# The residual sum of the attention split between ScalarE and POOL, with a new order of turn, copy and normalisation in each slot

## The reference

```
x = x + L0_xattn(layernorm(x), ctx, ctx)      # 16 heads of 8, biases, plain softmax
x = x + L0_ffn(layernorm(x))                  # 8 experts, each token goes to its top one
x = x + L1_xattn(layernorm(x), ctx, ctx)      # position bias per head, exp / (1 + sum)
x = x + L1_ffn(layernorm(x))                  # relu squared, two products, 5 spiking steps
```

## Time and profile before

| what | value |
|---|---|
| median of three executions | 414.28 us (412.43 to 416.89) |
| profiled execution | 411.08 us, span 409.3 us |
| TensorE matmul busy | 304.5 us, 74% |
| VectorE busy | 288.0 us, 70% |
| ScalarE busy | 253.5 us, 62% |
| POOL busy | 166.5 us, 41% |
| mean granted TensorE clock | 0.888 |

### The profile page before, as it was taken

One profiled execution on the slowest core, in us unless ns is written; L12 is line 12 of the kernel. 1 busy time (PEld: TensorE's weight loads), 2 busy tenths in 40 slices (PEclk: granted clock), 3 DMA queues, 4 the chain that ended last, 5 costly groups with the idle time before them and its releaser, 6 DMA issues.

```text
span 409.3 us, 9328 instructions
## 1 busy us (share of the span) xinstructions
PE 304.5 (74%) x3164; PEld 184.2 (45%) x3164; DVE 288.0 (70%) x713; ACT 253.5 (62%) x540; POOL 166.5 (41%) x304
## 2 busy tenths in 40 slices
PE   1579789888788717999921739878887787787783
PEld 0224334444333605999920214434343343476671
DVE  4788999999955583567523757978898583147884
ACT  2148888899884304555501238978888678657772
POOL 3314544647002018444037485557544211445500
PEclk9999999999996855999985556999999888989996
DMA  5234533333210504454112122112211100000001
GB/s 161 58 88 121 154 79 102 111 106 107 66 37 24 167 1 96 114 154 105 43 54 70 49 66 61 44 51 64 63 46 53 44 8 6 0 2 1 26 27 51
DMA packets 36207, 27.38 MB, mean 67 GB/s; under 512 B 6096, under 2 KB 32336, under 8 KB 36160
## 3 DMA queue, kind: packets, MB, share of 16 engines
q1 hardware_dynamic: 33040, 23.48, 20.2%
q0 software_dynamic: 1248, 2.56, 2.9%
q10 hardware_dynamic: 1872, 0.72, 0.7%
HBM read 14.22 MB, written 4.13 MB: 45 GB/s over the span
## 4 chain that ended last, share of the span: by engine, by line
PE 39%; DVE 24%; issue 9%; POOL 8%; ACT 8%; DMA 7%; SPq 3%; ACTq 1%; POOLq 0%; DVEq 0%
DVE nm L654 12%; PE M L355 7%; PE R L1257 6%; PE R L306 6%; PE R L1276 5%; ACT Pt L514 4%; DMA Qt<-mT 3%; DVE tmp L1389 2%; PE M L417 2%; DVE Pt L1392 2%; POOL w_ff L1173 2%; POOL xn L609 2%; SPq L878 1%; PE M L1445 1%; ACT Osb L500 1%
## 5 line engine op out<-in xcount | busy, mean ns | idle before, releaser
L654 DVE TENSOR_REDUCE nm<-R 128x2 f32<-128x512 f32 x256 | 164.7, 692 | 32.7 <-PE R L306 30.5
L514 ACT ACTIVATE Pt<-R 128x512 f32<-128x512 f32 x256 | 139.0, 596 | 29.8 <-PE R L315 27.7
L306 PE MATMUL R<-Kt,Qt 32*128 32x256 f16 x512 | 57.0, 304 | 25.5 <-DMA Qt<-q_hi 8.0
L355 PE MATMUL M<-Pt,Vt 128*32 128x256 f32 x1024 | 72.6, 403 | 3.8 <-DVE X L744 3.5
L315 PE MATMUL R<-Qt,Kt 32*128 32x256 f16 x512 | 54.3, 293 | 2.5 <-ACT Pt L514 2.3
L306 PEld LDWEIGHTS R<-Kt,Qt 32*128 32x128 f16 x512 | 15.6, 95 | 62.9 <-DVE nm L654 31.7
L355 PEld LDWEIGHTS M<-Pt,Vt 128*32 128x32 f32 x1024 | 27.6, 113 | 32.8 <-issue 9.8
L1304 ACT ACTIVATE hf<-R,b1c 128x128 f32<-128x128 f32 x92 | 26.2, 368 | 18.3 <-PE R L1257 18.0
L1166 POOL DMA_INDIRECT xt<-normed_x,source x23 | 22.5, 977 | 19.8 <-PE M L1267 14.9
L1257 PE MATMUL R<-x_t,w_t 128*128 128x128 f32 x184 | 28.0, 300 | 0.7 <-DVE x_t L1327 0.5
L1257 PEld LDWEIGHTS R<-x_t,w_t 128*128 128x128 f32 x184 | 24.7, 209 | 1.5 <-issue 1.2
(11 more groups left out here) (173 smaller groups left out, 545.7 us busy)
## 6 DMA issues: line engine op xcount, KB each, us to landing
w_ff<-in_w SPq DMA_DIRECT2D x8, 512.0 KB, 4.1
ctxT<-in_ctxT SPq DMA_DIRECT2D x16, 128.0 KB, 2.6
Pt<-in_mask SPq DMA_DIRECT2D x8, 256.0 KB
Qt<-q_hi SPq DMA_DIRECT2D x28, 64.0 KB, 2.4
Kt<-k_hi SPq DMA_DIRECT2D x28, 64.0 KB, 1.9
sorted_y<-ysb SPq DMA_DIRECT2D x23, 64.0 KB
Kt<-k_lo SPq DMA_DIRECT2D x16, 64.0 KB, 1.9
Qt<-q_const SPq DMA_DIRECT2D x16, 64.0 KB, 3.5
```

Of the source, the lines that this page charges most:

```text
L306: mm = pe.matmul(row_bank(b, h)[:, q, :], Qt[b % NBUF][rows_of(h), h // HG, q * P:(q + 1) * P], Kt[b % NBUF][rows_of(h), h // HG, :], star ...
L355: mm = pe.matmul(o_bank(b)[KB * i:KB * i + KB, tile * S:(tile + 1) * S], Vflat[par][:, at:at + KB], Pt[g][:, i, k * S:(k + 1) * S], start= ...
L514: act.activation(Pt[i // 2][:, 2 * j + hh, :], key_bank(b, 2 * i + hh).rearrange("p k n -> p (k n)"), ACT.Exp, scale=1.0 / SC).then_inc(ly ...
L654: v.tensor_reduce(nm[par][:, h // 8, :, h % HG, h // HG % 2], row_bank(b, h), AX.X, ALU.max, negate=True)\
```

## The change

- The sum into X is split. In slots in which batches s and s-1 both exist (s = 1 to 7), ScalarE copies M[1] into a new SBUF tile `op_out`, after the exponentials of pair 4 and before the copy of the values, and POOL adds `op_out` to X, after the keys' parts and before the norm. TensorE's `pv` waits for the copy (op_copied) rather than for the sum. In slot 8 VectorE adds as before.
- The turn of the maxima stands ahead of `pv` 0 on TensorE, and its copy on ScalarE stands between the two exponentials of pair 5.
- `o_norm` stands between the two reductions of pair 2 rather than behind them.
- In layer 0 `shift` becomes a tensor_tensor with a broadcast column of constants instead of a tensor_scalar.
- Consumers wait for the new places: VectorE's norm statistics of the last part wait for x_added; a semaphore nobody waited for (warmed) goes.

```
@@ constants
-    rows = np.zeros((P, 3), np.float32)
+    rows = np.zeros((P, 4), np.float32)
+    rows[:, 3] = 1.0 / MROW
@@ attention_on_tensor
                 pair(5)
+                if nxt:
+                    pe.wait_ge(ly["v_copied"], b + 2)
+                    m_turn(b + 1, par1, 0)
                 if cur:
                     if s == B - 1:
                         pe.wait_ge(ly["mT_copied"], 2 * B)
                     elif old:
-                        pe.wait_ge(ly["x_added"], b)
+                        pe.wait_ge(ly["op_copied"], b)
...
                     pv(b, par, 0)
-                if nxt:
-                    pe.wait_ge(ly["v_copied"], b + 2)
-                    m_turn(b + 1, par1, 0)
@@ attention_on_scalar
                 exp(4)
+                if old and cur:
+                    act.wait_ge(ly["op_done"], b)
+                    if older:
+                        act.wait_ge(ly["x_added"], b - 1)
+                    act.activation(op_out[:, :], M[1][:, 0:S], ACT.Copy).then_inc(ly["op_copied"], 1)
...
-                exp(5)
+                exp(5, (0,))
                 if nxt:
                     m_copy(b + 1, 0)
+                exp(5, (1,))
@@ attention_on_vector, shift
-                v.tensor_scalar(mparts..., nm..., 1.0 / MROW, None, ALU.mult)
+                v.tensor_tensor(mparts..., nm...,
+                                rows[:, 3:4].unsqueeze(1).to_broadcast([P, QT * HG, 2]), ALU.mult)
@@ attention_on_vector, slot
-                r(2)
+                r(2, (0,))
                 if old:
                     o_norm(b - 1)
+                r(2, (1,))
...
-                r(4)
-                if old:
+                r(4, (0,))
+                if old and not cur:
                     v.wait_ge(ly["op_done"], b)
+                    v.wait_ge(ly["x_added"], b - 1)
...
                     v.tensor_tensor(x, M[1][:, 0:S], x, ALU.add).then_inc(ly["x_added"], 1)
+                r(4, (1,))
@@ attention_on_gpsimd
+            def add_output(b):
+                pool.wait_ge(ly["op_copied"], b + 1)
...
+                x = X[:, b * QT:b * QT + QT, :].rearrange("p q d -> p (q d)")
+                pool.tensor_tensor(x, op_out[:, :], x, ALU.add).then_inc(ly["x_added"], 1)
...
                         key_rests_on_gpsimd(pool, ly, b, nxt)
+                if cur and old:
+                    add_output(b - 1)
                 if 0 <= s <= B - 4:
                     norm_root(pool, b + 3, ly["xvar"], ly["xrstd"])
@@ ffn_on_vector
                 if exists(s, 3):
+                    v.wait_ge(ly[1]["x_added"], s + 4 if s is not None and s < 2 else B)
```

More of the change, by code:

```diff
@@ L93, in layer @@
              "q_done", "q_copied", "k_done", "k_copied", "v_done", "v_copied", "q_hi", "q_lo",
-             "k_hi", "k_lo", "k_rep", "q_tile", "p1_done", "max_done", "m_parts", "own",
+             "k_hi", "k_lo", "k_rep", "q_tile", "p1_done", "max_done", "m_parts",
              "mT_done", "mT_copied", "m_rows", "p2_done", "exp_done", "pv_done", "o_copied", "ot_done",
-             "ot_norm", "o_rc", "aT_done", "aT_copied", "op_done", "x_added"]
+             "ot_norm", "o_rc", "aT_done", "aT_copied", "op_done", "op_copied", "x_added"]
     ly = {n: sem(f"L{index}_{n}") for n in names}
@@ L99, in layer @@
     if ly["position"]:
-        ly["k_pos"] = sem(f"L{index}_k_pos")
+        ly["own"], ly["k_pos"] = sem(f"L{index}_own"), sem(f"L{index}_k_pos")
     else:
@@ L122, in build @@
         eye16 = sb("eye16", [P, P], F16)
-        rows = sb("rows", [P, 3])
+        rows = sb("rows", [P, 4])
         W = {}
@@ L139, in build @@
         table_warm = sb("table_warm", [P, 1])
-        warmed = sem("warmed")
         xnT = sb("xnT", [P, S])
@@ L161, in build @@
         aT = sb("aT", [P, S])
+        op_out = sb("op_out", [P, S])
         R = psum("R", [P, 2 * RING, QT, S])
@@ L395, in slot_fn @@
                     if s == B:
-                        pe.wait_ge(ly["x_added"], B - 1)
+                        pe.wait_ge(ly["op_copied"], B - 1)
                     for n in range(QT * NPK):
@@ L504, in slot_fn, with exp @@
                 new, nxt, cur, old, older = (exists(s, d) for d in (2, 1, 0, -1, -2))
-                def exp(i):
+                def exp(i, heads=(0, 1)):
                     if not cur:
                         return
-                    if i % 2 == 0 and old:
+                    if i % 2 == 0 and old and heads[0] == 0:
                         act.wait_ge(ly["pv_done"], 4 * b - 3 + i // 2)
                     j = 1 - i % 2
-                    for hh in range(2):
+                    for hh in heads:
                         act.wait_ge(ly["p2_done"], H * b + 2 * i + hh + 1)
@@ L661, in shift @@
                     v.wait_ge(ly["mT_done"], 2 * b - 3 + half)
-                v.tensor_scalar(mparts[par][:, half, :, :, 0, :].rearrange("p q i g -> p (q i) g"),
-                                nm[par][:, half, :, :, :].rearrange("p q i g -> p (q i) g"), 1.0 / MROW, None, ALU.mult) \
+                v.tensor_tensor(mparts[par][:, half, :, :, 0, :].rearrange("p q i g -> p (q i) g"),
+                                nm[par][:, half, :, :, :].rearrange("p q i g -> p (q i) g"),
+                                rows[:, 3:4].unsqueeze(1).to_broadcast([P, QT * HG, 2]), ALU.mult) \
                  .then_inc(ly["m_parts"], 1)
@@ L686, in slot_fn, with r @@
                 ahead = s is None or s <= B - 4
[L688 to L691, removed]
+                def r(i, heads=(0, 1)):
+                    for hh in heads if nxt else ():
+                        reduce(b + 1, 1 - par, 2 * i + hh)
                 if cur and ly["bias"]:
@@ L800, in parts @@
                 pool.tensor_tensor(part[2], rest, part[1], ALU.subtract).then_inc(ly["m_parts"], 1)
+            def add_output(b):
+                pool.wait_ge(ly["op_copied"], b + 1)
+                if ly["bias"]:
+                    pool.wait_ge(ly["x_biased"], b + 1)
+                elif b < MIX:
+                    pool.wait_ge(moe["x"], b + 1)
+                else:
+                    pool.wait_ge(moe["mixed"], b - MIX + 1)
+                x = X[:, b * QT:b * QT + QT, :].rearrange("p q d -> p (q d)")
+                pool.tensor_tensor(x, op_out[:, :], x, ALU.add).then_inc(ly["x_added"], 1)
             def slot_fn(b, par, s):
-                new, nxt, cur = (exists(s, d) for d in (2, 1, 0))
+                new, nxt, cur, old = (exists(s, d) for d in (2, 1, 0, -1))
                 if cur and ly["position"]:
@@ L1460, in slot_fn @@
                 if s == -1:
-                    act.activation(table_warm[:, :], spike_bias[:, :], ACT.Sigmoid).then_inc(warmed, 1)
+                    act.activation(table_warm[:, :], spike_bias[:, :], ACT.Sigmoid)
                 if exists(s, -1):
@@ L1545, in _ @@
             act.wait_ge(inited, 1)
-            act.activation(table_warm[:, :], mhalf[:, 0:1], ACT.Exp).then_inc(warmed, 1)
+            act.activation(table_warm[:, :], mhalf[:, 0:1], ACT.Exp)
             act.wait_ge(inited, INIT_KEYS)
```

## The result

The changed kernel takes **418.44 us** (median of 18 runs, 414.86 to 422.04) against 413.59 for the kernel before on the same chip (18 runs, 410.05 to 416.89): ratio **1.0127, interval 1.0100 to 1.0153**, slower by about 5 us. The forecast was 412.2. Ratios leave out runs over 1.5% above the fastest of their kernel; medians hold all. The profiled execution took 419.71 us, with a span of 417.6 and a mean granted clock of 0.875 (before: 411.08, 409.3, 0.888).

The account below looks back on a forecast made before the run. No engine is full; TensorE's product 0 waits for VectorE's sum into X, queued behind ten reductions. Terms -1.5 - 1.2 + 0.5 + 0.1 = -2.1 us took the median 414.28 to 412.2 us, range 408.0 to 416.2.

Parts of the forecast that it names:

- POOL's add: POOL's queue: 0.72 us behind the keys' parts, hidden with 0.15 to spare; uncovered, up to 0.4 in each of six slots.
- the slots of layer 0: Layer 0's attention: five slots go from 12.53 to 12.22 us each, -1.5 us.
- the upper bound: Most that layer 0's five slots could gain, VectorE's sum and stalls both gone: 5 x (0.34 + 0.38) = 3.6 us.
- The scaling: Layer 0's scaling of the maxima on VectorE: as tensor_tensor it no longer waits for POOL's memset, -1.2 us.
- The turn ahead of product 0: TensorE: in layer 0 the turn waits for the values' copy, loop 12.22 us; in layer 1 the later product is hidden.
- Layer 1's other slots: Layer 1's attention: slots keep their length, since SyncE's queue sets the maxima's DMA; value 0.
- Slot 7 of layer 0: Before the gate: the sum comes 0.7 us later, of which 0 to 0.7 reaches the gate; +0.5 us taken.
- ScalarE did not become the bound: Rival, layer 0's slots: ScalarE's new copy delays the values' copy by 0.39, slots of 12.52 us; 415.9 us, chance 0.18.
- The stall did not stay: Rival, layer 0's scaling: the tensor_tensor still waits for the memset, the 1.2 us are gone; 413.4 us, chance 0.15.
- The clock in layer 1 did not hold: Rival, layer 1's slot 6: shifted queues avoid the long wait and low clock, 3.1 us more gained; 409.1 us, chance 0.22.
- The slower rival: The rival in which ScalarE becomes the bound: +1.6 us, 415.9 us, chance 0.18.

Follow-up runs that it names:

- b1: The kernel before with only layer 0's scaling of the maxima as a tensor_tensor: 413.72 us, ratio 0.9967.
- a1: The changed kernel with POOL making the parts of the maxima before its add in layer 1's slot 6: 413.71 us, ratio 1.0011.
- d2: a1 with the old order: turn behind product 0, copy of M[1] behind both exponentials; 416.10 us, ratio 0.9977.
- d4: The changed kernel with the old order of turn and copy of M[1], POOL's parts still late: 415.24 us, ratio 1.0081; again 418.20 us, 1.0113.
- c1: a1 with three groups of statistics ahead of the gate instead of two: 411.39 us, ratio 0.9909; again 410.36 us, 0.9932.
- a3: a1 with the sum of layer 0's slot 7 back on VectorE: 413.28 us, ratio 0.9989.
- g1: The kernel before with three groups of statistics ahead of the gate instead of two: 412.34 us, ratio 0.9975.

## Why the prediction was wrong

The sign was wrong, and the time lies outside the range. The step that failed is the one on POOL's add; the step on the slots of layer 0 was oversized as well. Step by step:

- **The slots of layer 0: the loop right, the saving mis-sized.** 12.22 us from pair 0 to pair 0, the values' copy at 8.28 us, no wait for X. But the -1.5 us took the new loop from 12.53, the mean of five slots with their disturbances, where the undisturbed slot before was 12.30. The disturbances stayed: slots with a wait of some 0.5 us for VectorE at pair 0 took 12.7 to 12.8, and one at low clock took 13.17. So the five slots behind the first took 0.6 us more in this profile instead of 1.5 less. Over the seven profiles with the moved sum and both new orders they took 61.4 to 64.3 us, mean 62.6, over the five with the old sum 62.6 to 63.9, mean 63.2: 0.6 us less, within the spread. The new order of the turn made the loop 12.22; without it it is 11.94. The 0.38 us of stalls in the upper bound stands in no row.
- **The scaling: right in kind.** 0.28 us at most, wait gone, the first slot 12.22 instead of 13.58. Of its 1.2 us the runs of b1 show 1.4, within an interval from -0.6 to 3.3.
- **POOL's add: the step that failed.** The prediction said that the add "stands after the keys' parts", that the parts of the maxima come behind with a wait to spare, and that it costs at most 0.4 us "in each of six slots". That reads only the slots with a new batch, in which the parts of half 0 stand ahead of the add and only those of half 1 behind it. In slot 6 of layer 1 there is no new batch, the program takes another branch, and there parts(b+1, half 0) stands behind add_output(b-1), which waits for ScalarE's copy at 336.25. The parts came 2.4 us late, the granted clock of the stretches behind was 0.50 and 0.54, and putting them first again gave 4.8 us back (a1), not 0 and not 0.4. The bound was wrong because the add was priced by its length, 0.72 us, where what stands behind it pays for its wait as well.
- **The turn ahead of product 0: half read.** I asked what it waits for in layer 0. In layer 1 it also waits for POOL's parts, and once they are late, it holds product 0 and all that TensorE has behind it. In d2 and d4 slot 6 is without that, but d4's time stays at 1.008 to 1.011, so how much of the loss is the turn's is open.
- **Layer 1's other slots: right where they were undisturbed.** 13.15 and 13.16 us for slots 2 and 3 (before 13.14 and 13.13). Slots 1, 4, 5 and 7 moved by -0.6, +0.4, -1.5 and +0.9 us; they differ by as much among profiles of kernels that are alike there.
- **Slot 7 of layer 0: the delay right, its price open.** +0.5 taken, the sum 0.7 later. The normalisation ahead of the gate begins 13.51 us after Osb 7, against 12.67 in b1, which has the old sum: 0.8 us. What that costs was asked of the chain alone. In the profile the gate ends 2.9 us later, at half clock, and three groups of statistics cure it (c1). But a gate at half clock behind a fast slot 7 also stands in b1 and a3, which have no moved sum there, so that this loss belongs to the moved sum is not shown; putting the sum back gave 0.9 to 1.6 us, within the intervals. That a1 stays at 1.001 instead of the 0.995 of the forecast (2.1 us of 411) is in part the missing saving of layer 0's slots, 0.9 us by the means above; the rest lies within a1's interval.
- **The rivals.** ScalarE did not become the bound. The stall did not stay. The clock in layer 1 did not hold: slot 6 began after a wait of 1.44 us instead of 1.87, and the clock then fell for longer. The slower rival had the sign, but for another reason.

## What to carry to other kernels

- An operation moved to an in-order queue costs the wait that it brings, and not only its length, to all that stands behind it (here a wait of 8.12 us for an add of 0.72). Go through every branch of that engine's program, the first and last slots above all, and write down what is behind the moved operation in each.
- Price a shortened loop against an undisturbed turn of the same loop, not against the mean: what disturbs the others may stay. Here 12.30 to 12.22 was real and 12.53 to 12.22 was not.
- A wait moved ahead in one engine can meet a late producer in another: slot 6 was 16.59 us with both and 14.45 with the late parts alone. Where an edit moves a consumer forward, look at all its producers in all the layers that run this code.
- A gain ahead of a stage whose input comes from another engine can end as a wait there; look at the chain to that input before counting the gain. Here, with POOL's parts first, a split of the statistics took the kernel from 1.001 to 0.991 and 0.993.

## What the runs showed of the hardware

- **VectorE beside POOL.** In the rows read here the scaling ends with POOL's instruction or is not held at all. As tensor_scalar it began in the last 0.5 us of POOL's sum, and was held to 43.76, past the end of the memset behind that sum, at 43.73: 2.27 us. In g1 it began inside the memset and took 1.63 us, to 43.83, with the memset's end at 43.79. As tensor_tensor it took 0.18 in the middle of the memset, and 0.54 beside POOL's sum, ending at 55.41 with that sum's end at 55.38 (b1). The same place three slots later has both kinds, a POOL sum and a memset of 0.95 us behind it: the tensor_scalar took 1.41 us, to the memset's end (before, at 80.10), the tensor_tensor 0.52, to the sum's end (b1, at 80.01). The Trainium skill (SBUF — State Buffer, Who interferes with whom) has it so: an exclusive lock, which an operation with two SBUF inputs meets only where the GpSimd instruction reads SBUF. The traces agree in these rows. The row at 370.98 does not fit a whole lock: that operation with two SBUF inputs ended at 371.54, and POOL's normalisation beside it, begun at 370.77, at 371.62. The prediction took less than a whole wait from it, and for the scaling the wait was whole.
- **The granted clock after an idle stretch.** Nearly the same code, the same busy share, another outcome: from 120 to 124 TensorE was busy 2.48 of 4 us in both kernels; before, the clock was at 0.85 in that stretch and 0.50 in the next, and in the changed kernel it stayed at 1.00 up to 132 and was at 0.51 in the stretch with the 2.58 us wait. The same slot took 10.36 or 13.25 us. The length of the wait does not decide it: ahead of the gate the clock fell after 2.58 us (changed), 0.78 (a3) and 0.23 (b1), each behind a slot 7 of under 12 us. So a single profile can move several microseconds from one stage to the next, and only sums over both, or many profiles, compare kernels here.
